# A windowed-attention block on one core: other PSUM banks for V and the output, another order on ScalarE and GpSimd, another order of the MLP's transfers

## The reference, cut to what matters

```python
xs = jnp.roll(x, shift=(-4, -4), axis=(1, 2))
win = xs.reshape(B, H // 8, 8, W // 8, 8, C).transpose(0, 1, 3, 2, 4, 5).reshape(-1, 64, C)
h = _ln(win, ln1_g, ln1_b)
q, k, v = (jnp.einsum('ntc,chd->nthd', h, w) + b for w, b in ((wq, bq), (wk, bk), (wv, bv)))
attn = jax.nn.softmax(jnp.einsum('nqhd,nkhd->nhqk', q, k) / np.sqrt(32), axis=-1)
o = jnp.einsum('nhqk,nkhd->nqhd', attn, v)
win = win + jnp.einsum('nqhd,hdc->nqc', o, wo) + bo
h2 = _ln(win, ln2_g, ln2_b)
win = win + jax.nn.gelu(h2 @ w1 + b1, approximate=False) @ w2 + b2
# windows back to the image, rolled by (4, 4)
```

## Time and profile before

| | before |
|---|---|
| median of 3 runs | 5499.32 us (5499.07 to 5499.84) |
| the profiled execution's own time | 5499.27 us |
| its span | 5495.1 us, mean granted TensorE clock 0.976 |
| TensorE matmul, weight load | 4849.6 us (88%), 4009.3 us (73%) |
| VectorE, ScalarE, GpSimd | 4037.0 us (73%), 3956.6 us (72%), 3805.3 us (69%) |
| DMA | 622.24 MB, 113 GB/s |

### The profile page before, as it was taken

The page is one execution under the profiler, slowest core; times in us unless marked ns, Lnnn a source line. Parts: engine busy times, 40 slices in busy tenths (PEclk is TensorE's granted clock), DMA queues, the critical chain, the costliest instruction groups (busy, mean ns, idle before and its releaser), DMA issues.

```text
span 5495.1 us, 291417 instructions
## 1 busy us (share of the span) xinstructions
PE 4849.6 (88%) x109308; PEld 4009.3 (73%) x109308; DVE 4037.0 (73%) x9010; ACT 3956.6 (72%) x8309; POOL 3805.3 (69%) x4329
## 2 busy tenths in 40 slices
PE   6898889899898888988989888898988989888888
PEld 4777777777777777777777777777777777777777
DVE  7868768687686876868767687776877768677686
ACT  6877667686676767768677686776867677676776
POOL 6767757677575876757767577675776757767576
PEclk9999999999999999999999999999999999999999
DMA  4353433434334243343433434234342343523334
GB/s 122 112 149 95 121 104 96 145 90 122 104 99 139 89 131 102 104 132 93 133 93 112 127 92 141 87 111 126 91 144 88 114 121 89 151 88 115 112 93 148
DMA packets 443044, 622.24 MB, mean 113 GB/s; under 512 B 46009, under 2 KB 352538, under 8 KB 442586
## 3 DMA queue, kind: packets, MB, share of 16 engines
q1 hardware_dynamic: 441024, 617.92, 37.9%
q10 hardware_dynamic: 1562, 0.50, 0.0%
HBM read 309.96 MB, written 308.28 MB: 113 GB/s over the span
## 4 chain that ended last, share of the span: by engine, by line
PE 23%; DVE 20%; issue 17%; ACT 17%; DMA 9%; SPq 6%; POOL 5%; ACTq 2%; DVEq 1%; POOLq 0%
PE psum L732 8%; DVE row_max L1012 5%; DMA turned_rows<-probs 4%; PE psum L684 4%; ACT hT_upper L788 4%; DVE stats L958 3%; SPq L276 3%; PE psum L718 3%; DMA oT<-turned_rows 3%; PE psum L655 3%; POOL rstd L425 2%; DVE probs L1019 2%; DVE normed L1055 2%; PE psum L608 2%; PE psum L641 2%
## 5 line engine op out<-in xcount | busy, mean ns | idle before, releaser
L385 POOL TENSOR_TENSOR probs<-probs,prob_inv 128x512 f32<-128x512 f32 x771 | 782.7, 1044 | 1042.0 <-DVE prob_inv L1035 1042.0
L1041 DVE TENSOR_TENSOR stream<-stream,psum 128x384 f32 (+1 forms) x1024 | 551.3, 549 | 783.9 <-PE psum L684 484.8
L777 ACT ACTIVATE normed<-stream,shift,rstd 128x96 f32 (+1 forms) x2176 | 809.4, 462 | 76.5 <-POOL shift L434 43.0
L806 ACT ACTIVATE gelu_odd<-psum 128x512 f32<-128x512 f32 x768 | 403.5, 597 | 553.5 <-PE psum L655 553.4
L425 POOL TENSOR_TENSOR rstd<-variance,minus_half 128x16 f32<-128x16 f32 (+2 forms) x249 | 781.5, 3138 | 20.2
L684 PE MATMUL psum<-wo_w,oT 128*64 128x96 f32 x8192 | 460.4, 256 | 337.4 <-ACT v L811 337.2
L958 DVE BATCH_NORM_STATS2 stats<-stream 128x6 f32 (+2 forms) x4224 | 716.8, 243 | 42.2 <-DVE stream L1041 20.4
L684 PEld LDWEIGHTS psum<-wo_w,oT 128*64 128x64 f32 x8192 | 362.6, 139 | 422.7 <-ACT v L811 385.5
L732 PE MATMUL psum<-w_w,gelu_odd 128*64 128x96 f32 x12288 | 566.9, 255 | 112.8 <-ACT gelu_odd L860 112.7
L732 PEld LDWEIGHTS psum<-w_w,gelu_odd 128*64 128x64 f32 x12288 | 543.1, 143 | 162.7 <-issue 162.7
L732 PEld LDWEIGHTS psum<-w_w,gelu_even 128*64 128x64 f32 x12288 | 535.6, 142 | 125.5 <-issue 125.5
(11 more groups left out here) (99 smaller groups left out, 11078.6 us busy)
## 6 DMA issues: line engine op xcount, KB each, us to landing
turned_rows<-probs SPq DMA_DIRECT2D x624, 128.0 KB
turned_rows<-probs SPq DMA_DIRECT2D x208, 384.0 KB, 2.8
stream<-in_x SPq DMA_DIRECT2D x272, 192.0 KB, 3.1
h_raw_even<-turned_rows SPq DMA_DIRECT2D x390, 128.0 KB
h_raw_odd<-turned_rows SPq DMA_DIRECT2D x387, 128.0 KB
out<-stream SPq DMA_DIRECT2D x256, 192.0 KB
stream<-in_x SPq DMA_DIRECT2D x272, 180.0 KB
out<-stream SPq DMA_DIRECT2D x256, 180.0 KB
```

Of the source, the lines that this page charges most:

```text
L385: nc.gpsimd.tensor_tensor(block_h, block_h, inv, ALU.mult).then_inc(probs_ready, 1)
L777: last = nc.scalar.activation(normed1[:, t, :], stream[:, slot, t * C:(t + 1) * C], ACT.Identity, bias=shift1[:, index, t:t + 1], scale=rs ...
L1041: nc.vector.tensor_tensor(part, part, psum[:, banks[g], 0:GROUP], ALU.add).then_inc(added, 1)
```

## The change

V and the two output halves get other PSUM banks, and the waits that guard the banks follow. ScalarE's copy of the next unit's rows is cut into two halves that stand apart: the first ahead of q and k of the second token half, the second behind the V copies; the exponentials move too. GpSimd makes the first lower half ahead of the normalising of the probabilities. In the MLP step ScalarE does both gelu groups first, then half of `normalise1`, `copy_h2T_upper`, and the other half. VectorE adds the first output half ahead of its lower rows. In the transfers the fetch goes behind the first three store DMAs, and `send_h1` goes last.

```diff
@@ -150,8 +150,8 @@
...
         PV_BANKS = (3, 6)
-        V_BANKS = (6, 5)
-        O_BANKS = (3, 6)
+        V_BANKS = (5, 6)
+        O_BANKS = (2, 3)
...
@@ -268,11 +268,11 @@
...
-            def store(row, half):
+            def store(row, half, which=slice(None)):
...
                 slot = (2 * row + half) & (SLOTS - 1)
-                for dram, sbuf in dram_and_sbuf(out_rows, row, half, slot):
+                for dram, sbuf in list(dram_and_sbuf(out_rows, row, half, slot))[which]:
                     sp.dma_start(dram, sbuf).then_inc(stored, 16)
...
@@ -323,10 +323,12 @@
...
                     send_turned(batch + i + 4, turned_late, n)
-                    store(batch_row + i // 2, i % 2)
+                    store(batch_row + i // 2, i % 2, slice(0, 3))
+                    fetch_late(batch + i + 4, n)
+                    if i % 2:
+                        store(batch_row + i // 2, 1, slice(3, 6))
                     if i >= 2:
                         send_h1(batch + BATCH + i + 1, turned1_late)
-                    fetch_late(batch + i + 4, n)
                 for i in range(BATCH - 4, BATCH):
...
@@ -384,14 +386,13 @@
...
-            def copy_hT_lower(u, parity):
+            def copy_hT_lower(u, parity, g):
                 upper, lower = [half[0:C, :] for half in hT_split]
-                for g in range(2):
-                    tokens = slice(g * SHARES, (g + 1) * SHARES)
-                    pool.wait_ge(hT_upper_copied, 2 * u + g + 1)
-                    nc.gpsimd.tensor_tensor(lower[:, tokens], h_raw[parity][0:C, tokens], upper[:, tokens],
-                                            ALU.subtract).then_inc(hT_copied, 1)
+                tokens = slice(g * SHARES, (g + 1) * SHARES)
+                pool.wait_ge(hT_upper_copied, 2 * u + g + 1)
+                nc.gpsimd.tensor_tensor(lower[:, tokens], h_raw[parity][0:C, tokens], upper[:, tokens],
+                                        ALU.subtract).then_inc(hT_copied, 1)
...
@@ -511,10 +512,12 @@
...
                         finish2(next(calls), 4, 4, 2)
+                    if s >= -3:
+                        copy_hT_lower(s + 3, (s + 3) % 2, 0)
                     if s >= -1:
...
                     if s >= -3:
-                        copy_hT_lower(s + 3, (s + 3) % 2)
+                        copy_hT_lower(s + 3, (s + 3) % 2, 1)
                 return next(calls)
...
@@ -543,8 +546,9 @@
...
                         lower_early(b, batch + 1, 1, copy_h2T_early(batch + 1, 1))
+                    copy_hT_lower(batch + s + 3, (s + 3) % 2, 0)
                     normalise_probs(batch + s + 1, (s + 1) % 2)
-                    copy_hT_lower(batch + s + 3, (s + 3) % 2)
+                    copy_hT_lower(batch + s + 3, (s + 3) % 2, 1)
                 return call + 6
...
@@ -614,9 +618,9 @@
...
                     if g == 0:
+                        need(shift_done, HEADS * (u - 1) + 2)
+                    else:
                         need(oT_copied, 2 * (u - 1))
-                    else:
-                        need(shift_done, HEADS * (u - 1) + 2)
                     for t in range(TILES // 2):
...
@@ -629,7 +633,7 @@
...
                 pe.wait_ge(qk_copied, 4 * (u + 1))
-                need(v_copied, 2 * (u + 1))
+                need(v_copied, 2 * u + 1)
                 need(shift_done, HEADS * u)
...
@@ -646,11 +650,12 @@
...
                 if h == 0:
-                    pe.wait_ge(qk_copied, 4 * (u + 1) + 2)
+                    wait_apart(pe, qk_copied, 4 * (u + 1) + 2)
+                    pe.wait_ge(attn_added, 2 * u + 1)
                 elif h == 1:
...
                 else:
-                    pe.wait_ge(attn_added, 2 * u + 1)
+                    pe.wait_ge(attn_added, 2 * u + 2)
                 for quad in range(QUADS):
...
@@ -660,7 +665,7 @@
...
                 wait_apart(pe, pt_copied, HEADS * (u + 1))
-                wait_apart(pe, attn_added, 2 * u + 2)
+                wait_apart(pe, v_copied, 2 * (u + 2))
                 for quad in range(QUADS):
...
@@ -675,9 +680,8 @@
...
                 if g == 0:
+                    wait_apart(pe, qk_copied, 4 * (u + 2) + 2)
                     pe.wait_ge(oT_copied, 2 * (u + 1))
-                else:
-                    pe.wait_ge(v_copied, 2 * (u + 2) + 1)
                 for t in range(TILES // 2):
...
@@ -767,26 +771,28 @@
...
-            def normalise1(u, index):
-
-                wait_apart(act, rstd1_ready, u + 1)
-                if not (isinstance(u, int) and u == 0):
-                    wait_apart(act, h1_turned, u)
+            def normalise1(u, index, tiles=range(TILES)):
+
+                if tiles[0] == 0:
+                    wait_apart(act, rstd1_ready, u + 1)
+                    if not (isinstance(u, int) and u == 0):
+                        wait_apart(act, h1_turned, u)
                 slot = u % SLOTS if isinstance(u, int) else u & (SLOTS - 1)
-                for t in range(TILES):
+                for t in tiles:
                     last = nc.scalar.activation(normed1[:, t, :], stream[:, slot, t * C:(t + 1) * C], ACT.Identity,
                                                 bias=shift1[:, index, t:t + 1], scale=rstd1[:, index, t:t + 1])
-                last.then_inc(ln1_ready, 1)
-
-            def copy_hT_upper(u, parity):
-
-                act.wait_ge(h1_back[parity], 8 * CBLOCKS * (u - parity) + 16 * CBLOCKS)
+                if tiles[-1] == TILES - 1:
+                    last.then_inc(ln1_ready, 1)
+
+            def copy_hT_upper(u, parity, g):
+
+                if g == 0:
+                    wait_apart(act, h1_back[parity], 8 * CBLOCKS * (u - parity) + 16 * CBLOCKS)
                 if not (isinstance(u, int) and u == 0):
-                    act.wait_ge(qk_done, 4 * u)
-                for g in range(2):
-                    tokens = slice(g * SHARES, (g + 1) * SHARES)
-                    nc.scalar.activation(hT_split[0][0:C, tokens], h_raw[parity][0:C, tokens], ACT.Copy)\
-                        .then_inc(hT_upper_copied, 1)
+                    act.wait_ge(qk_done, 4 * (u - 1) + 2 * g + 2)
+                tokens = slice(g * SHARES, (g + 1) * SHARES)
+                nc.scalar.activation(hT_split[0][0:C, tokens], h_raw[parity][0:C, tokens], ACT.Copy)\
+                    .then_inc(hT_upper_copied, 1)
...
@@ -832,24 +838,25 @@
...
                         copy_probsT(back, h)
+                if not absent(middle):
+                    exps(middle, 1 - half, 0)
                 if not absent(front):
...
                 if not absent(middle):
-                    exps(middle, 1 - half, 0)
+                    exps(middle, 1 - half, 1)
                 if not absent(back):
...
                 if not absent(middle):
-                    exps(middle, 1 - half, 1)
                     exps(middle, 1 - half, 2)
+                copy_hT_upper(u + 3, 1 - half, 0)
                 if not absent(front):
...
                     copy_qk(front, 3)
-                copy_hT_upper(u + 3, 1 - half)
-                if not absent(front):
                     copy_v(front, half, 0)
                     copy_v(front, half, 1)
+                copy_hT_upper(u + 3, 1 - half, 1)
...
@@ -910,23 +917,25 @@
...
-                def mlp_step(j, odd):
+                def mlp_step(j, odd, norm):
                     gelus(batch + j, odd, 1)
+                    gelus(batch + j + 1, 1 - odd, 0)
+                    if norm:
+                        normalise1(batch + BATCH + j + 1, j + 1, range(TILES // 2))
                     copy_h2T_upper(batch + j + 2, odd)
-                    gelus(batch + j + 1, 1 - odd, 0)
+                    if norm:
+                        normalise1(batch + BATCH + j + 1, j + 1, range(TILES // 2, TILES))
...
                 for j in (0, 1):
-                    mlp_step(j, j)
+                    mlp_step(j, j, False)
                 with act.Fori(1, BATCH // 2 - 1) as k:
                     for odd in (0, 1):
-                        j = 2 * k + odd
-                        mlp_step(j, odd)
-                        normalise1(batch + BATCH + j + 1, j + 1)
+                        mlp_step(2 * k + odd, odd, True)
                 gelus(batch + BATCH - 2, 0, 1)
+                gelus(batch + BATCH - 1, 1, 0)
                 normalise1(batch + 2 * BATCH - 1, BATCH - 1)
-                gelus(batch + BATCH - 1, 1, 0)
                 gelus(batch + BATCH - 1, 1, 1)
...
@@ -1079,11 +1088,11 @@
...
-            def add_mlp(u):
-                dve.wait_ge(b2_added, u + 1)
-                for g in range(2):
-                    dve.wait_ge(down_done, 2 * u + g + 1)
-                    add_into_stream(u, DOWN_BANKS, g, mlp_added)
+            def add_mlp(u, g):
+                if g == 0:
+                    dve.wait_ge(b2_added, u + 1)
+                dve.wait_ge(down_done, 2 * u + g + 1)
+                add_into_stream(u, DOWN_BANKS, g, mlp_added)
...
@@ -1165,8 +1174,9 @@
...
```

(16 more changed lines are left out.)

## The result

The changed kernel takes 5573.76 us (median of 4 runs, 5572.67 to 5576.71), against 5499.58 us for the kernel before in the same job: a ratio of 1.0136, 95% interval 1.0124 to 1.0148. It is 74 us slower. I had forecast 5387 us, with slower at 0.09.

The account below looks back on a forecast made before the run. Bounds were bank-order waits in attention (V copy) and a two-step chain through h1's DMA in the MLP, no full engine. 16 x (-11.6 + 4.6) = -112 us from 5499.27 gave 5387 us, range 5275 to 5495.

Parts of the forecast that it names:

- -11.6 us a batch: Attention stage: net gain from the vanished V copy wait and an earlier first step, less what is given back.
- the first step: Attention: the stall on returning rows stays, but scores start 1.0 us sooner.
- give-backs: Attention, per batch: 2.4 us through normalise1 on ScalarE, 2.3 through GpSimd's queue, 0.5 through extra statistics on VectorE.
- my own signs: Prediction wrong if transposes wait for L385 or L1041, h1 turns wait no longer, or landing is far from 3.4 us.
- rival 4: Attention: GpSimd's earlier lower half delays probabilities; TensorE waits 0.4 us in 15 steps, 6 us more; 5483 us, chance 0.09.
- 6.6: MLP queue: h1 sent behind the fetch costs four pairs 1.64 us each, +6.6 us a batch.
- a pair of 21.0 us: MLP two-step chain with h1 behind the fetch, odd iteration: 10.2 to send, 3.4 landing, 6.0, 0.3 and 1.08 us.
- the landing: MLP queue: time from h1's issue to VectorE's turn of h1, taken as 3.4 us, from 2.7 to 5.2.
- rival 2's toll: MLP: VectorE and GpSimd's shared port costs 2.3 us in every pair; pair 21.6, total 5474 us, chance 0.13.
- Rival 3: MLP queue: h1 behind the fetch lands in 5.2 us, even chain 23.4 us; total 5541 us, chance 0.08.
- 0.3 us in the two-step chain: MLP, ScalarE: cost of half of normalise1 ahead of h2T_upper, from 0 to 1.5 us.
- 2 us a batch: MLP: gain from the odd iteration's earlier fetch and gelus freeing TensorE, from 0 to 8 us.

Follow-up runs that it names:

- first run: Kernel before with the attention part of the change alone, the MLP's three orders as before: 5353.64 us, 0.9718.
- second run: Changed kernel with all of normalise1 behind the rows' copy (h2T_upper), both gelu groups still leading: 5404.84 us, 0.9825.
- fifth run: The second run with h1 sent before the fetch, which still lies between the stores: 5282.13 us, 0.9604.
- third run: Changed kernel with the old transfer order (send h2, store, send h1, fetch), half of normalise1 still ahead: 5532.73 us, 1.0052.
- run 4: Changed kernel with normalise1 behind h2T_upper and the transfers in the old order; leading gelus and early add remain: 5321.71 us, 0.9676.
- run 9: Changed kernel with GpSimd finishing the MLP statistics, and so the shift, ahead of its lower half: 5508.58 us, 1.0011.
- run 7: Changed kernel with half of normalise1 ahead of h2T_upper only in the even MLP steps: 5583.93 us, 1.0154.
- run 6: Changed kernel with half of normalise1 ahead of h2T_upper only in the odd MLP steps: 5489.42 us, 0.9973.
- run 12: Changed kernel with only the send of h1 moved ahead of the fetch, half of normalise1 still ahead: 5537.18 us, 1.0055.
- run 8: Run 4 with VectorE's order as before, both adds behind its lower half: 5358.73 us, 0.9741.
- run 11: The first run with the fifth run's queue alone (send h1, fetch, rest of the store): 5319.85 us, 0.9664.

## Why the prediction was wrong

**Attention: right, and somewhat too high.** I had -11.6 us a batch; the stage gave -9.1. The wait for the V copy went, the first step kept its stall (scores wait for V 5.40 us in the trace after), and of the give-backs the one through GpSimd was seen in the wait list above: the transposes wait for the probabilities 150 times, 49.7 us in all, 3.1 us a batch against my 2.3 for its queue. By my own signs that wait of the transposes counts against the forecast and for rival 4, at half the 6 us that rival 4 has for it. Another 1.55 us is TensorE's busy time in the stage, 163.19 against 161.64 us for the same 4992 instructions, which I had not in the sum. The rest of the difference I did not take apart. The first run confirms the part as a whole: 5354 us, as its stage length said.

**The queue: right in mechanism, the size partly by luck.** Over the whole run h1 behind the fetch costs 122 us (second and fifth runs), 7.6 us a batch; I had 6.6. I had a pair of 21.0 us with h1 sent behind the fetch. The second run, in which this is the bound, has 20.7 on average, and the fifth, without it, 19.28, the 19.36 of before. But its pairs are not alike. The four with a turn of h1 in them have 19.74, 21.78, 19.85 and 20.15 us; the first, which I had left at 19.36, has 21.88. The one of 21.78, by SyncE's queue and VectorE:

```profile
2966.93 1.77 SPq L282 DMA_DIRECT2D turned_rows<-probs  x3
...
2976.74 0.41 SPq L300 DMA_DIRECT2D turned_rows<-probs  x1
```

```profile
2979.51 0.98 DVE L1012 STREAM_TRANSPOSE probs<-normed 128x768 f32<-128x768 f32 x1 [2.93 <-DMA turned_rows<-probs]
...
2983.20 2.23 DVE L1062 TENSOR_TENSOR normed<-stream,mean 128x768 f32 x1
2985.55 1.83 DVE L1069 TENSOR_TENSOR normed<-normed,rstd 128x768 f32<-128x768 f32 x1
2987.62 0.98 DVE L1079 STREAM_TRANSPOSE probs<-normed 128x768 f32<-128x768 f32 x1 [0.25 <-DVE normed L1069]
```

From send to send it is 9.81 us (I had 10.2), then 2.77 to the turn of h1 (I had 3.4), then 8.11 to the next turn of h2 (I had 6.0), since centring and scaling took 2.23 and 1.83 us here and not 0.96 each. In the other three pairs this last stretch is 5.9 to 6.0 us. So the landing was too long in my sum and the meeting with GpSimd, rival 2's toll, was missing from it in one pair of four, and the two errors pull in opposite ways; the four pairs average 20.38 us. Rival 3, on the slower side like the result, is not what happened: it wanted a landing of 5.2 us, while the landings of the second run's stage are 2.5 to 3.9 us.

**ScalarE's order in the MLP: the failed step.** It is the sentence "half of 2.98 us then lies ahead of the copy that VectorE's lower half awaits: 0.3 us in the two-step chain, from 0 to 1.5". I named the wait for the turn of h1, but priced only the instructions that lie ahead of the copy, not what they wait for. And I did not name the wait for GpSimd's shift at all: normalise1 waits for `rstd1_ready` before anything else. In the trace before, both waits were short (43.0 us for the shift and 29.2 us for the turn in the whole run), and normalise1 stood behind everything urgent, so that lateness cost nothing. The fifth run shows that: it waits 149.5 us for the shift and is the fastest. In front of the rows' copy they cost 3.1% with the new queue and 3.8% with the old (runs 2 to 4). The half alone took a pair from 20.7 to 22.86 us, where I had 0.3 for it.

Why so much: the shift follows GpSimd's lower half of the rows before, which follows ScalarE's copy of those. With the half ahead, the next copy follows the shift. A chain that led out of the loop became part of it; where the long statistics call stands in it, it is 23.44 us for two steps. Run 9 opens this ring or, behind the long call, shortens it, and gets 69 of 171 us back; run 7 shows that the even steps, where the shift is new, suffice for the whole loss. The ring through the turn of h1 and its DMA was seen above in an even step, at 23.33 us; that the same ring makes the 1.5% of the odd steps alone (run 6) is argued, not shown. How the two share the loss when both are there I can't say: they overlap, and where the one is shortened the other takes its place (runs 3, 9 and 12).

**What I priced at nothing.** I gave the leading gelus and the earlier fetch 2 us a batch, 32 us in all; the leading gelus by themselves show nothing (runs 1 and 8), the fetch 30 to 40 us (runs 1 and 11, 4 and 5). The early add, for which I had "nothing", is worth 36 us (run 8). It lets the first half be added ahead of the lower rows. That it works through the down bank is argued, not shown.

**The sum.** Attention as measured (-9.1) and the queue as predicted (+4.6) would have given about 5430 us. The missing term is the half of normalise1, +171 us by run 2. That gives about 5600, some 25 us more than measured, and the early add, 36 us by run 8, is missing from it with the other sign. That the term of normalise1 was missing could be seen in the kernel's text: a wait ahead of the moved instructions, whose releaser depends on the instruction they were put in front of.

The best version is the fifth run: banks and attention orders as in the change, both gelu groups first, normalise1 wholly behind the rows' copy, the early add, and h1 sent ahead of a fetch that lies between the stores.

## What to carry to other kernels

When instructions move ahead of an urgent one in an in-order engine, their waits move with them. Price each wait by when its releaser will be done, not by its idle time in the old profile: that is what was left when the engine got there late, and it was harmless only because nothing urgent stood behind it. Then follow the releaser back: if it depends on the instruction that was overtaken, a ring has been closed. In a DMA queue a step that waits for a landing belongs behind the issues that another engine will soon wait for, as h1 here; the rest of the store, which nobody waits for so soon, lost nothing behind it. And a change of many parts is to be run part by part: this one showed a loss of 1.4%, while its parts with two of them put elsewhere (normalise1 and h1's send) gain 4.0%.

## What the runs showed of the hardware

I had not expected the clock to follow so small a change: TensorE's granted clock over one MLP stage was 0.94 in the changed kernel and 0.97 in the second run, at 22.86 and 20.7 us a pair. Behind five of the six waits for even lower rows in the changed kernel's stage the matmuls ran at the lower of the two levels, 0.63 us each instead of 0.39: behind those of 2.98, 3.61 and 3.75 us from the first on, behind those of 4.75 and 2.24 us from the third on. Behind the wait of 3.23 us all ran at the upper level. So a late operand can cost on TensorE twice, by the wait and behind it, but the length of the wait alone does not tell when: in the third run's stage TensorE waits in the same even steps, and the clock is 0.97. The 1825 matmul instructions of the changed kernel's stage took 146.55 us instead of 139.37.
